# Gate weights before the inverse denominators, and their transposes and copy moved up, in phase two of a graph transformer layer

## Chip, core and metric

The kernel runs on one core of a Trainium2 chip. The metric is the device time of one launch in microseconds (us).

## What is computed

The reference is one layer over 12,500 nodes of 256 channels, with 12,500 of the edges used. Cut to what matters here:

```python
xn = layernorm(x)
x  = x + graph_attention(xn, edges) + linear_attention_mix(xn)      # elu+1 features, message, W1, relu, W2, layernorms
z  = layernorm(x)
gates = softmax(z @ gW + gb)                                         # 4 experts
topv, topi = top_k(gates, 2); topw = softmax(topv)                   # weights of the 2 kept experts
out = x + shared_mlp(z) + sum(topw * expert_mlp(z)[topi])
```

In the mix part each of 8 heads divides by a denominator, the dot product of its query features with the sum of its key features.

## The kernel before

Rows are handled in 25 groups of 500 nodes (`NG`, `GR`; 125 partitions by `T` = 4). Phase one (until about 250 us) builds the key/value sums and a table of transformed rows in DRAM. Phase two goes over the groups in a software pipeline, written out by hand for each engine as `phase2(i, par, a, b, c)`. In step i, part `a` is the attention part of group i, part `b` is W1 and W2 of the mix for group i-1, and part `c` is the feed-forward part (shared network, four experts, gates) of group i-2. All three run in steps 2 to 24; step 25 has b and c, step 26 has c alone. Steps 3 to 24 are mostly a hardware loop of two steps a turn. Each engine runs its own instructions in order, and only semaphores tie the engines together. Matrix products are split into three fp32r matmuls (L222 to L224), a high by high, a high by low and a low by high one; the "low" tiles (`h_lo`, `e_lo`, `s_lo`, `z_lo`) are subtractions, most of them on GpSimd (POOL) through the helper `low` (L1349).

The names that matter:

- **VectorE (DVE)**, part a and c of a step in this order: `p2_feature` (L1007, L1009), the softmax inputs (`soft_chain_in`), `compare` (ranks the four gate logits, L1092 to L1099), `soft_chain_out` (L1079 to L1083, signals `gates`), `one_over_den` (L1126 to L1132: add epsilon, reciprocal, split in two, signals `den_rows`), `top_weights` (L1108 to L1120: mask the exponentials, sum, reciprocal, multiply, split, write to `scale_rows`, signals `gate_rows`), row statistics `bn_y` (L902), the product of the query features with the inverse denominators (L1203, signals `q_den`), their low part `z_lo` (L1207), and later the product of the expert outputs with the expanded gates (L1217).
- **ScalarE (ACT)**: relu passes (L789, L790) of the four experts, then the exponential `top_exp` of the gates (L859), the high part `z_hi` of the scaled query features (L863, waits for `q_den`), the relu passes of `s2` (L789, L790; signals `s2_relu`), and for the two halves of the experts' second layer a relu (L873); `copy_scales` (L795, PSUM to `scaleT`) stands between these two.
- **TensorE (PE)**: `p2_den` (L492, denominators), W2 in two pairs of tiles (`w2_pair`), the expansion of the inverse denominators (L638, waits for `den_rows`), sW2, the first half of eW2, the four transposes of `scale_rows` (`transpose_scales`, L564, waits for `gate_rows`), the second half of eW2, the expansion of the gates (L662, waits for `scaleT` and `s2_relu`), the message matmuls (wait for `qz`, that is for `z_lo`), half of W1 for the next step, and the output matmuls.
- **POOL**: gathers of table rows (L1343, L1345), `h_lo`, `s_lo`, a sum into `base`, more gathers, `e_lo` for two pairs of experts, `s_lo` for s2, and small statistics.

The order on VectorE before:

```python
soft_chain_out(i, a, c)
if a: one_over_den(i)
if c: top_weights(i)
```

Of the kernel before, what the change touches and what calls it, by code (L numbers as in the profile page):

```python
# [53 lines left out]
def gps_layer(nc, A):  # L54

    ctx = ExitStack()
    with ctx:
# [353 lines left out]
        def _(pe):  # L411
# [144 lines left out]
            def phase2(i, par, a=True, b=True, c=True, started=False):  # L556
# [3 lines left out]
                def transpose_scales():  # L560
                    if due(i - 1):
                        pe.wait_ge(S["gate_rows"], i - 1)
                    for j in range(T):
                        last = pe.transpose(psum[:, 5, j * R:(j + 1) * R], scale_rows[:, j, :], ident[0:R, 0:R])  # L564
                    last.then_inc(S["scale_t"], 1)
# [65 lines left out]
                if b:  # L631
                    for pair in range(2) if c else (1,):
                        w2_pair(i, pair, c)
                if a:
                    pe.wait_ge(S["den_rows"], i + 1)
                    for q in range(CK):
                        for j in range(T):
                            last = pe.matmul(psum[:, 6 + q, j * P:j * P + R + 1], den_sel[:, q, j, :], rdenT[:],  # L638
                                             start=True, stop=True)
                        last.then_inc(S["dx"], 1)  # L640
                if c:
                    if due(i - 1):
                        pe.wait_ge(S["s1_lo"], i - 1)
                    if due(4 * (i - 1)):
                        pe.wait_ge(S["e1_relu"], 4 * (i - 1))
                    hidden("sW2", 0, 0, 4, (s1_hi, s1_lo)).then_inc(S["s2_mm"], 1)
                    for q in range(2):
                        if due(2 * (i - 2) + q + 1):
                            pe.wait_ge(S["e1_lo"], 2 * (i - 2) + q + 1)
                        for m in range(2):  # L650
                            e = 2 * q + m
                            last = split_mm(pe, colT(2 + q), (wslice(w_hi, "eW2", e), wslice(w_lo, "eW2", e)),
                                            (e1_hi[:, e, :], e1_lo[:, e, :]), m == 0, m == 1)
                        last.then_inc(S["e2_mm"], 1)
                        if q == 0:
                            transpose_scales()
                    if due(i - 1):
                        pe.wait_ge(S["scaleT"], i - 1)
                    if due(i - 1):
                        pe.wait_ge(S["s2_relu"], i - 1)  # L660
                    for q in range(2):
                        last = pe.matmul(colT(4 + q), gate_sel[:, q, :], scaleT[:], start=True, stop=True)  # L662
                    last.then_inc(S["gb"], 1)
# [46 lines left out]
        def _(act):  # L710
# [91 lines left out]
            def phase2(i, par, a=True, b=True, c=True, started=False):  # L802
                if b:
                    if due(i):
                        act.wait_ge(S["mt"], i)
                    act.activation(mT_hi[:], colT(0, 2), ACT.Copy).then_inc(S["mT_hi"], 1)
                if c:
                    if due(i - 1):
                        act.wait_ge(S["rs_z"], i - 1)
                    if due(i - 2):  # L810
                        act.wait_ge(S["zt"], i - 2)
                    normalize(row_z, lambda j: xmid[par][:, j, :], LZ, "z_norm")
                if b:
                    if due(i - 2):
                        act.wait_ge(S["e2_lo"], i - 2)
                for o in range(2):
                    if b:
                        relu_split(relu[0][:, o, :], h_hi[:, o, :], 4 + o, h_bias[:, o:o + 1],
                                   4 * (i - 1) + o + 1, "h_mm", "h_relu")
                    if c and o == 0:  # L820
                        if due(i - 1):
                            act.wait_ge(S["zt"], i - 1)
                        act.activation(z_hi[:], colT(0, 2), ACT.Copy).then_inc(S["z_hi"], 1)
                if b:
                    if due(2 * (i - 2)):
                        act.wait_ge(S["e1_lo"], 2 * (i - 2))
                    for o in range(2, 4):
                        relu_split(relu[1][:, o - 2, :], h_hi[:, o, :], 4 + o, h_bias[:, o:o + 1],
                                   4 * (i - 1) + o + 1, "h_mm", "h_relu")
                if c:  # L830
                    if due(i - 2):
                        act.wait_ge(S["s2_lo"], i - 2)
                    for o in range(2):
                        relu_split(relu[2][:, o, :], s1_hi[:, o, :], 5 if o == 0 else 0, s1_bias[:, o:o + 1],
                                   2 * (i - 2) + o + 1, "s1_mm", "s1_relu")
                        if o == 0:
                            act.wait_ge(S["lg_mm"], i - 1)
                            act.activation(logitsT[:], colT(1), ACT.Copy).then_inc(S["lg"], 1)
                if a and not started:
                    p2_exp(i)  # L840
                if c:
                    for e in range(EXPERTS):
                        if e == 0:
                            if b:
                                act.wait_ge(S["h_lo"], 2 * (i - 1) + 1)
                            else:
                                act.wait_ge(S["e2_lo"], i - 2)
                        if e == 2:
                            if b:
                                act.wait_ge(S["h_lo"], 2 * (i - 1) + 2)  # L850
                            else:
                                act.wait_ge(S["e1_lo"], 2 * (i - 2))
                        relu_split(relu[e // 2][:, e % 2, :], e1_hi[:, e, :], 1 + e, e1_bias[:, e:e + 1],
                                   4 * (i - 2) + e + 1, "e1_mm", "e1_relu")
                        if e == 2:
                            soft_exp(i, a, c)
                    if due(i - 1):
                        act.wait_ge(S["gates"], i - 1)
                    act.activation(top_e[:], soft_e[:, 0, :, :], ACT.Exp).then_inc(S["top_exp"], 1)  # L859
                if a:  # L860
                    for q in range(CK):
                        act.wait_ge(S["q_den"], 2 * i + q + 1)
                        act.activation(z_hi[:, q, :], qf[:, q, :], ACT.Copy).then_inc(S["qz_hi"], 1)  # L863
                if c:
                    if due(i - 1):
                        act.wait_ge(S["s1_lo"], i - 1)
                    relu_split(relu[2][:, 0, :], s2_hi[:], 4, s2_bias[:, 0:1], i - 1, "s2_mm", "s2_relu")
                    if due(2 * (i - 2) + 1):
                        act.wait_ge(S["e1_lo"], 2 * (i - 2) + 1)
                    for q in range(2):  # L870
                        if due(2 * (i - 2) + q + 1):
                            act.wait_ge(S["e2_mm"], 2 * (i - 2) + q + 1)
                        act.activation(relu[0][:, q, :], colT(2 + q), ACT.Relu,  # L873
                                       bias=e2_bias[:, q:q + 1]).then_inc(S["e2_relu"], 1)
                        if q == 0:
                            copy_scales(i)
                    for q in range(2):
                        if due(2 * (i - 2) + q + 1):
                            act.wait_ge(S["e2g"], 2 * (i - 2) + q + 1)
                        act.activation(h_hi[:, q, :], relu[0][:, q, :], ACT.Copy).then_inc(S["e2_hi"], 1)  # L880
                if a:
                    act.wait_ge(S["rs_m"], i + 1)
                    normalize(row_n, lambda j: rowt(6, j), LM, "m_norm")
                if a and not c:
                    soft_exp(i, a, c)
# [11 lines left out]
        def _(dve):  # L897
# [269 lines left out]
            def phase2(i, par, a=True, b=True, c=True, more=True, started=False):  # L1167
# [14 lines left out]
                if c:  # L1182
                    soft_chain_in(i, par, a, c)
                    dve.drain()
                    compare(i)
                    soft_chain_out(i, a, c)
                if a:
                    one_over_den(i)
                if c:
                    top_weights(i)  # L1190
                if b:
                    if due(2 * i - 1):
                        dve.wait_ge(S["w2"], 2 * i - 1)
# [240 lines left out]
```

## Time and profile before

| | |
|---|---|
| median of 3 runs | 1503.72 us (1503.57 to 1506.25) |
| profiled execution, own time | 1505.46 us |
| its span, first to last instruction | 1503.7 us |
| TensorE clock granted, mean | 0.986 |
| busy: PE / DVE / ACT / POOL | 1414.6 / 1151.3 / 759.2 / 953.5 us |
| DMA, mean over the span | 81 GB/s |

Read the rows this way: in a timeline row the numbers in front are the start and the time of the group in us from the span's start; "x2" is how many instructions the row merges; the brackets give how long the engine had been idle before and which instruction released it. TensorE matmuls overlap, so a row's duration is longer than the distance to the next one, and the distances are what counts.

### The profile page before, as it was taken

The page shows a single profiled execution, that of the slowest core. Times are in us where ns is not written, and L with a number is a line of the kernel's source. Part 1 is how long each engine was busy: PE and PEld are TensorE (multiplying, and loading weights), DVE is VectorE, ACT ScalarE, POOL GpSimd, SP SyncE. Part 2 cuts the span into 40 slices and gives each one's busy share as a digit, 9 for nine tenths or more (in the row PEclk, how much of TensorE's full clock was granted, in tenths as well). Part 3 has the DMA queues.
Part 4 walks back from the last instruction along what each step waited for, and adds up shares of the span by engine and source line. Part 5 has one row for each costly group of instructions (what it writes and reads, how often), then busy time and mean ns, then how long its engine had stood idle before and what let it go on. Part 6 is the DMA issues. An engine that isn't in the chain of part 4 may idle for free.

```text
span 1503.7 us, 26952 instructions
## 1 busy us (share of the span) xinstructions
PE 1414.6 (94%) x9032; PEld 1279.9 (85%) x9032; DVE 1151.3 (77%) x2565; ACT 759.2 (50%) x1339; POOL 953.5 (63%) x873
## 2 busy tenths in 40 slices
PE   5999999679999999999999999999999999999986
PEld 5999999568888888888888888888888888888875
DVE  6777778558878878787788877788777887878873
ACT  4555555235554445644556445554455445554453
POOL 5777775566775666656676567755677556675452
PEclk9999999899999999999999999999999999999998
DMA  5787765121220212202122112211122111220000
GB/s 175 254 266 230 226 217 194 53 60 49 70 70 23 64 52 69 65 24 62 56 69 62 28 48 69 69 41 48 48 69 69 31 55 52 69 67 24 14 14 14
DMA packets 71630, 121.81 MB, mean 81 GB/s; under 512 B 38053, under 2 KB 42786, under 8 KB 71598
## 3 DMA queue, kind: packets, MB, share of 16 engines
q1 hardware_dynamic: 55598, 108.00, 22.7%
q0 software_dynamic: 16000, 13.43, 4.1%
q8 instruction: 14, 0.23, 0.1%
q14 instruction: 18, 0.15, 0.0%
HBM read 69.47 MB, written 51.70 MB: 81 GB/s over the span
## 4 chain that ended last, share of the span: by engine, by line
PE 62%; DVE 21%; ACT 6%; issue 5%; DVEq 4%; POOL 1%; POOLq 1%; DMA 0%; SPq 0%; ACTq 0%
PE psum L222 18%; PE psum L224 18%; PE psum L223 18%; DVE top_e L1108 6%; PE psum L419 4%; DVE qf L1007 2%; DVE qf L1203 2%; ACT qf L775 2%; DVEq L1056 2%; DVE psum L1128 1%; PE psum L662 1%; ACT relu L789 1%; ACT relu L873 1%; ACT s_hi L790 1%; DVE bn_y L902 1%
## 5 line engine op out<-in xcount | busy, mean ns | idle before, releaser
L1349 POOL TENSOR_TENSOR s_lo<-relu,s_hi 128x1000 fp32r<-128x1000 f32 (+1 forms) x50 | 89.9, 1797 | 150.5 <-ACT s_hi L790 150.5
L222 PE MATMUL psum<-w_hi,h_hi 128*125 128x256 f32 x600 | 172.5, 287 | 5.1 <-DVE h_lo L1229 3.7
L224 PE MATMUL psum<-w_hi,h_lo 128*125 128x256 f32 x600 | 170.1, 283 | 0.0
L223 PE MATMUL psum<-w_lo,h_hi 128*125 128x256 f32 x600 | 169.6, 283 | 0.0
L1343 POOL DMA_INDIRECT xg<-table_xt,idx x100 | 124.7, 1247 | 55.1 <-issue 55.1
L863 ACT ACTIVATE z_hi<-qf 128x500 fp32r<-128x500 f32 x50 | 30.2, 622 | 232.2 <-DVE qf L1203 224.3
L1349 POOL TENSOR_TENSOR h_lo<-relu,h_hi 128x1000 fp32r<-128x1000 f32 x50 | 127.4, 2567 | 29.8 <-ACT h_hi L790 29.8
L1146 DVE SCALAR_TENSOR_TENSOR base<-xb,rn,b_bc 125x256 f32<-125x256 f32 x100 | 144.6, 1486 | 0.3
L1345 POOL DMA_INDIRECT ag<-table_al,idx x100 | 121.3, 1213 | 30.5 <-issue 30.5
L222 PE MATMUL psum<-z_hi,w_hi 128*128 128x500 f32 x300 | 119.8, 399 | 2.3 <-DVE z_lo L1177 2.3
L222 PE MATMUL psum<-xT_hi,w_hi 128*128 128x500 f32 x300 | 120.5, 402 | 1.3 <-ACT h_hi L790 1.3
L1349 POOL TENSOR_TENSOR e_lo<-relu,e_hi 128x1000 fp32r<-128x1000 f32 x50 | 116.1, 2348 | 3.3 <-ACT e_hi L790 2.7
L223 PE MATMUL psum<-xT_lo,w_hi 128*128 128x500 f32 x300 | 117.8, 393 | 0.0
L224 PE MATMUL psum<-xT_hi,w_lo 128*128 128x500 f32 x300 | 117.5, 392 | 0.0
L223 PE MATMUL psum<-z_lo,w_hi 128*128 128x500 f32 x300 | 117.4, 391 | 0.0
L222 PEld LDWEIGHTS psum<-w_hi,h_hi 128*125 128x125 f32 x600 | 112.2, 187 | 6.0 <-DVE h_lo L1229 4.1
L224 PE MATMUL psum<-z_hi,w_lo 128*128 128x500 f32 x300 | 116.9, 390 | 0.0
L714 ACT ACTIVATE row_n<-psum,nm_m,rs_m 125x256 f32<-125x256 f32 x100 | 48.4, 565 | 131.4 <-POOL nm_m L1286 131.4
L224 PEld LDWEIGHTS psum<-w_hi,h_lo 128*125 128x125 f32 x600 | 112.9, 188 | 0.0
L223 PEld LDWEIGHTS psum<-w_lo,h_hi 128*125 128x125 f32 x600 | 112.9, 188 | 0.0
L1108 DVE SCALAR_TENSOR_TENSOR top_e<-rank,top_e 125x16 f32<-125x16 f32 x25 | 91.3, 3650 | 4.4 <-issue 3.8
L1319 POOL TENSOR_TENSOR k_lo<-kf,k_hi 125x1024 fp32r<-125x1024 f32 x25 | 63.0, 2521 | 40.7 <-DVE k_hi L956 40.7
(231 smaller groups left out, 4754.1 us busy)
## 6 DMA issues: line engine op xcount, KB each, us to landing
xb<-in_x SPq DMA_DIRECT2D x50, 448.0 KB
xT_hi_table<-x1T_hi SPq DMA_DIRECT2D x25, 500.0 KB
xT_lo_table<-x1T_lo SPq DMA_DIRECT2D x25, 500.0 KB
xT_hi<-xT_hi_table SPq DMA_DIRECT2D x25, 500.0 KB
xT_lo<-xT_lo_table SPq DMA_DIRECT2D x25, 500.0 KB
table_xt<-xts SPq DMA_DIRECT2D x25, 455.0 KB
out<-xmid SPq DMA_DIRECT2D x25, 448.0 KB
xb<-in_x SPq DMA_DIRECT2D x50, 52.0 KB
```

The lines of the kernel that those rows point to most:

```text
L222: pe.matmul(out, wh, xh, start=first, stop=False)
L223: pe.matmul(out, wh, xl, start=False, stop=False)
L224: return pe.matmul(out, wl, xh, start=False, stop=last)
L419: last = pe.transpose(psum[:, b + c, j * R:(j + 1) * R], src[:, j, c * P:(c + 1) * P], ident[0:R, 0:R])
L714: act.activation(out[:, j, :], src(j), ACT.Identity, bias=nm[which][:, j:j + 1], scale=rs[which][:, j:j + 1]).then_inc(S[done], 1)
L863: act.activation(z_hi[:, q, :], qf[:, q, :], ACT.Copy).then_inc(S["qz_hi"], 1)
L1108: stt(top_e[:], rank[:], float(TOPK), top_e[:], ALU.is_lt, ALU.mult)
L1146: last = stt(base[:, j, :], xb[par][:, j, :], rn2[par][:, 0, j:j + 1], b2_bc[:], ALU.mult, ALU.add)
L1319: ptt(k_lo[par][:], kf[par][:], k_hi[par][:], ALU.subtract).then_inc(S["k_split"], 1)
L1343: pool.indirect_dma_start(xg[par][:, j, :], None, table_xt.ap(), bass.IndirectOffsetOnAxis(idx[par][:, 1, j:j + 1], 0)).then_inc(S[f"gath{ ...
L1345: pool.indirect_dma_start(ag[par][:, j, :], None, table_al.ap(), bass.IndirectOffsetOnAxis(idx[par][:, 0, j:j + 1], 0)).then_inc(S[f"gath{ ...
L1349: ptt(out, src, hi, ALU.subtract).then_inc(S[done], 1)
```

## The change

Three things move in phase two, and nothing is added or taken away. On VectorE `top_weights` comes right behind `soft_chain_out` and ahead of `one_over_den`. On TensorE the four transposes of the gate rows move from between the two halves of eW2 to right behind W2, ahead of the wait for `den_rows`. On ScalarE the copy of the transposed rows moves from between the two relus of the experts' second layer to right behind the exponential of the gates, ahead of `z_hi`.

```diff
@@ TensorE, phase2
                     for pair in range(2) if c else (1,):
                         w2_pair(i, pair, c)
+                if c:
+                    transpose_scales()
                 if a:
                     pe.wait_ge(S["den_rows"], i + 1)
@@
                         last.then_inc(S["e2_mm"], 1)
-                        if q == 0:
-                            transpose_scales()
@@ ScalarE, phase2
                     act.activation(top_e[:], soft_e[:, 0, :, :], ACT.Exp).then_inc(S["top_exp"], 1)
+                if c:
+                    copy_scales(i)
                 if a:
                     for q in range(CK):
                         act.wait_ge(S["q_den"], 2 * i + q + 1)
@@
                                        bias=e2_bias[:, q:q + 1]).then_inc(S["e2_relu"], 1)
-                        if q == 0:
-                            copy_scales(i)
@@ VectorE, phase2
                     soft_chain_out(i, a, c)
+                    top_weights(i)
                 if a:
                     one_over_den(i)
-                if c:
-                    top_weights(i)
```

## Rows read from the trace of the kernel before

**Rows 1.** Page, part 4: the chain that ended last, shares by engine and line.

```profile
PE 62%; DVE 21%; ACT 6%; issue 5%; DVEq 4%; POOL 1%; POOLq 1%; DMA 0%; SPq 0%; ACTq 0%
```

**Rows 2.** Waits of PE from 240 us to the end: total us, times, longest.

```profile
PE psum L662 <- ACT scaleT L795: 34.3, 23, 1.5
```

**Rows 3.** Timeline of PE in one step, from the end of W2.

```profile
977.17 1.01 PE L638 MATMUL psum<-rdenT,den_sel 128*128 128x126 f32 x8
978.01 0.44 PE L222 MATMUL psum<-s_hi,w_hi 128*128 128x500 f32 x1
...
980.77 0.59 PE L564 MATMUL psum<-ident,scale_rows 125*128 125x125 f32 x4
...
982.33 0.39 PE L224 MATMUL psum<-e_hi,w_lo 128*128 128x500 f32 x1
984.26 0.72 PE L662 MATMUL psum<-scaleT,gate_sel 128*128 128x500 f32 x2 [1.54 <-ACT scaleT L795]
984.83 0.28 PE L222 MATMUL psum<-g_hi,z_hi 128*125 128x256 f32 x1
```

**Rows 4.** Timeline of DVE in the same step.

```profile
970.49 0.19 DVE L1083 TENSOR_TENSOR soft_e<-soft_e,soft_s 125x32 f32<-125x32 f32 x1
971.67 0.30 DVE L1126 TENSOR_SCALAR psum<-psum 128x125 f32<-128x125 f32 x1 [0.99 <-issue]
...
973.43 0.29 DVE L1132 TENSOR_TENSOR rdenT<-psum,rdenT 64x125 fp32r<-64x125 f32 x1
973.91 4.12 DVE L1108 SCALAR_TENSOR_TENSOR top_e<-rank,top_e 125x16 f32<-125x16 f32 x1 [0.18 <-issue]
...
979.26 0.17 DVE L1120 TENSOR_TENSOR scale_rows<-top_e,top_hi 125x16 f32<-125x16 f32 x1
...
980.13 1.24 DVE L1203 TENSOR_TENSOR qf<-qf,psum 128x500 f32<-128x500 f32 x2
```

**Rows 5.** Timeline of ACT in the same step.

```profile
971.02 0.21 ACT L859 ACTIVATE top_e<-soft_e 125x16 f32<-125x16 f32 x1
980.83 1.21 ACT L863 ACTIVATE z_hi<-qf 128x500 fp32r<-128x500 f32 x2 [9.59 <-DVE qf L1203]
981.94 0.67 ACT L789 ACTIVATE relu<-psum,s_bias 128x500 f32<-128x500 f32 x1
...
983.62 0.59 ACT L795 ACTIVATE scaleT<-psum 128x500 fp32r<-128x500 f32 x1
```

**Rows 6.** Timeline of POOL in the same step.

```profile
973.33 4.66 POOL L1349 TENSOR_TENSOR e_lo<-relu,e_hi 128x1000 fp32r<-128x1000 f32 x2
983.24 1.24 POOL L1349 TENSOR_TENSOR s_lo<-relu,s_hi 128x500 fp32r<-128x500 f32 x1 [5.26 <-ACT s_hi L790]
```

**Rows 7.** Line L1108 over the whole kernel: duration in ns, min/median/max.

```profile
L1108 DVE SCALAR_TENSOR_TENSOR top_e<-rank,top_e x25: 174/4117/4218, 356.1 to 1483.3; 125x16 f32<-125x16 f32 x25
```

**Rows 8.** Timeline of POOL and DVE beside a gather in the next step.

```profile
997.75 1.33 POOL L1343 DMA_INDIRECT xg<-table_xt,idx  x1 [0.60 <-issue]
...
998.56 1.05 DVE L1160 TENSOR_SCALAR gnn<-xg,soft_e,rn 125x64 f32<-125x64 f32 x4
```

**Rows 9.** Timeline of DVE and PE in steps 24, 25 and 26.

```profile
1402.24 0.19 DVE L1083 TENSOR_TENSOR soft_e<-soft_e,soft_s 125x32 f32<-125x32 f32 x1
...
1404.91 1.01 PE L638 MATMUL psum<-rdenT,den_sel 128*128 128x126 f32 x8
...
1447.17 0.39 PE L222 MATMUL psum<-s_hi,w_hi 128*128 128x500 f32 x1
...
1449.46 0.17 DVE L1120 TENSOR_TENSOR scale_rows<-top_e,top_hi 125x16 f32<-125x16 f32 x1
...
1485.92 0.96 PE L564 MATMUL psum<-ident,scale_rows 125*128 125x125 f32 x4 [2.29 <-DVE scale_rows L1120]
...
1489.19 0.76 PE L662 MATMUL psum<-scaleT,gate_sel 128*128 128x500 f32 x2
```

**Rows 10.** Busy times in a window: PE, PEld, DVE, ACT, POOL, granted clock, DMA.

```profile
1486.50:1489.20 2.70, 2.70 (x9) 2.19 (x8) 0.00 (x0) 0.59 (x1) 0.00 (x0) 0.50 0.00 0
```

## The prediction

> **What bounds the kernel now.** I read the page's chain first: TensorE holds 62% of it and VectorE 21% [rows 1]. So the end is set by TensorE for most of each step and by a chain on VectorE for the rest. I then asked the waits of PE alone, over the whole of phase two. One wait stands out: L662, the expansion of the gates, waits for `scaleT`, 23 times, 34.3 us in all [rows 2]. Last came one step on every engine. From the first L1108 at 356.1 to the one shown at 973.91 there are 13 steps, 47.5 us each [rows 4, 7], and they repeat within hundredths of a microsecond, so one step stands for 22 of them (2 to 23).
>
> On PE the step runs without a gap until the last eW2 matmul at 982.33; L662 comes at 984.26 and the message matmuls at 984.83 [rows 3]. Twelve matmuls of the same size take 980.77 - 978.01 = 2.76, or 0.23 each. Without a wait the message would begin at 982.33 + 3 x 0.23 = 983.02. The wait thus costs 984.83 - 983.02 = 1.8 us a step, a little more than the 1.54 in brackets, which counts from the modelled end of the last matmul.
>
> What is late is a chain on VectorE. L1108 works on 16 elements and takes 4.12 us [rows 4]; its median over 25 is 4117 ns and its minimum 174 [rows 7]. The engine does not need that time. It begins at 973.91, inside the two `e_lo` subtractions of POOL, which run from 973.33 to 977.99, and ends at 978.03 [rows 4, 6]. So an instruction of VectorE with two SBUF operands stands still while POOL subtracts. L1132, which has one operand in PSUM, starts at 973.43, inside the same subtraction, and takes 0.29 [rows 4]: it is not held. Behind L1108 come the rest of `top_weights` (until 979.26 + 0.17 = 979.43), `bn_y` and L1203 at 980.13 [rows 4]. ACT waits 9.59 us for L1203, then does `z_hi`, the relus of s2, a relu of e2 and last the copy of the scales from 983.62 to 984.21 [rows 5]. That releases L662.
>
> **The VectorE order.** L859 ends at 971.23 [rows 5]. `top_weights` can start 0.03 later, at 971.26. L1108 unblocked takes 0.17 [rows 7], and from its end to the end of L1120 it is 979.43 - 978.03 = 1.40 [rows 4]. That gives 972.83, which is 0.50 before `e_lo` starts at 973.33 [rows 6]. Both sides keep this distance: POOL and VectorE are both set off by TensorE's work earlier in the step, of which nothing changes. So the 4.1 us stall goes. `one_over_den` then runs from 972.85 and needs 973.72 - 971.67 = 2.05: `den_rows` comes at 974.9 instead of 973.7. It now lies beside `e_lo`, but none of its four instructions reads two SBUF operands, and L1132 shows such a one unheld. TensorE asks for it after W2 and the moved transposes, at 977.57, so 2.7 us of slack cover it. If the cover were gone, each microsecond of lateness would cost one.
>
> Row and rule: the stall row above fits what the Trainium skill says (page "SBUF — State Buffer", section "Who interferes with whom"): VectorE instructions with two SBUF inputs contend with a GpSimd instruction that reads SBUF, and the one that started first goes through. The same section also speaks against the change: casts and copies in SBUF in a two-port mode take the pair as well and can collide with GpSimd's writing of DMA descriptors, and the moved L1116 and L1119 are such. The page gives no price for a 16-element copy.
>
> From rows: `top_weights` will now run beside the gathers that end just before `e_lo`. No row has a copy beside a gather; the nearest is L1160, SBUF to SBUF, four in 1.05 us beside a gather of 1.33 [rows 8], so about 0.26 each. The bound from below is nothing, and from above one gather of 1.33 for the copies. I take nothing; the upper bound is the rival below.
>
> **The moved transposes and copy.** They wait for `gate_rows` (972.83), long past when PE reaches them at 977.17. Between 980.77 and the last eW2 matmul at 982.33 lie the transposes and five spacings, so they take 1.56 - 5 x 0.23 = 0.4 of PE's time, wherever they stand [rows 3]. The expansion of the denominators moves from 977.17 to 977.57. L1203 can start when half of it is through and has landed: 977.57 + 0.42 (half of the 0.84 to sW2) + about 0.3 = 978.3 instead of 980.13. The copy on ACT (0.59) fits at 977.8 to 978.4 in a 9.59 us idle stretch [rows 5]; behind its wait stands only `z_hi`, which needs L1203 anyway. `z_hi` follows L1203 by 0.70 as now: 979.0. The relus of s2 follow that by 1.11 and take 2 x 0.67 at most: `s2_relu` at 981.4 [rows 4, 5]. PE asks for it at 982.56, 1.1 us later. `z_lo` goes behind `z_hi` (until 980.2) half by half and ends about 980.9; PE wants it at 983.0. `s_lo` on POOL, which waits for `s2_relu` [rows 6], would start near 981.4, after `z_lo`, so these two don't meet. So L662 follows the last eW2 matmul directly. The later part of the step hangs on PE and shifts as a whole. No DMA issue is moved, and SP's and POOL's queues are passed by nothing. Gathers and loads have a step of slack.
>
> Sum for steps 2 to 23: 22 x -1.8 = -40 us. With only the bracketed 1.54 won it is -34.
>
> **The last three steps pay.** Step 24: POOL has no gathers there, `e_lo` runs early and delays the softmax instead, L1083 ends at 1402.43 [rows 9]. `gate_rows` comes at 1402.43 + 0.3 + 1.6 = 1404.3 and `den_rows` 2.05 later, at 1406.3, while PE is ready at 1404.91 + 0.4. It waits 1.0 there and loses its old wait at L662, the twenty-third of them (34.3 - 22 x 1.53 = 0.6, and 0.3 more as above): +0.1. Step 25: PE reaches sW2 at 1447.17, but the transposes now stand in front and `gate_rows` comes at 1449.63 [rows 9]: PE waits 2.5 us, +2.5, as the rest of the tail hangs on eW2. Step 26: the transposes wait until 1485.92 already, but with 12 matmuls done before. Now these come behind. From the transposes to L662 there were 3.27 us for 4 transposes and 6 matmuls at a clock of 0.50, its lower level of 1.2 GHz [rows 9, 10]. At the upper level the same takes 0.4 + 6 x 0.23 = 1.8. With 18 matmuls it is 4.5 at the upper level and 4.5 x 3.27 / 1.8 = 8.2 at the lower. So L662 moves by +1.2 to +4.9; the output matmuls behind it may give back up to 1.5 where the clock has risen by then. I take +2.5, nearer to the row with the low clock. Together +5, from +1.5 to +8; should the clock fall in step 25 too, 18 matmuls there at twice the spacing add 4.
>
> **Sum.** -40 + 5 = -35 us. Against the profiled execution's own 1505.46 that gives 1470.5. That execution lay 1.7 above the median of the runs, so I put the median at **1469 us**, -2.3%.
>
> **Rivals.**
>
> *POOL gets the port first (slower).* If one of L1108 to L1120 is still to start when `e_lo` does at 973.33, it stands until 977.99. The margin is 0.67 for the start of L1120 (972.66). The copies held by a gather, up to 1.33, would use it up. Then `gate_rows` comes at 978.2, the transposes end at 978.6, `den_rows` comes at 980.25, the expansion starts at 980.3 and sW2 at 981.15. Eighteen matmuls bring PE to L662 at 985.3 and two more spacings to the message at 985.75, against 984.83: +0.9 a step, x 22 = +20, +5 for the tail: 1529. For it: the margin is thin, and no row has copies beside gathers. Against it: L1160 beside one, and steps that repeat so closely. Chance 0.08.
>
> *A second wait takes over.* L662 or the message could find `s2_relu` or `z_lo` late, if L1203 is held or starts later than I put it. From 1.1 us of lateness it costs; with 2 us a step it takes 0.8 of the 1.8 and leaves -22 + 5: 1487. Against it: the brackets of ACT show idleness before `z_hi` [rows 5]. Chance 0.08.
>
> *It doesn't do what it says.* If the 4 us belong to the first instruction that waits for `top_exp`, and not to POOL, the stall moves with it: L1108 would end at 975.4, `den_rows` comes at 975.4 + 1.4 + 2.05 = 978.85, and PE waits 1.3 there in place of 1.8 at L662: 22 x -0.5 + 5 = -6, 1498. The minimum of 174 ns [rows 7] speaks against it. Chance 0.04.
>
> **Numbers.** A change under 0.2% (3 us) can't be told from none here. My forecast has 0.80, its own range 1465 to 1482: -34 + 12 above, -40 + 1.5 below. To hold 8 in 10 I reach towards the second-wait case: 1461 to 1487. Faster 0.88, same 0.03, slower 0.09.
>
> **What would show it.** Right: L1108 at 0.17 us in steps 2 to 23, L662 without idle time before it, steps 45.7 us apart, L638 0.4 later relative to W2, a new PE wait at L564 near 2.5 us in step 25 and one at L638 in step 24. Wrong: a DVE line of 4 us elsewhere in `top_weights`, PE idle before L564 or L638 in every step, or a low clock through more of the tail.

## The result: slower by 2.6%, and what the profile after shows

| | before | changed |
|---|---|---|
| median | 1503.67 us (4 runs, 1503.57 to 1506.25) | 1543.58 us (4 runs, 1541.8 to 1545.52) |
| ratio, 95% interval | | 1.0261 [1.0244, 1.0279] |
| span of the profiled execution | 1503.7 us | 1541.5 us |
| mean granted TensorE clock | 0.986 | 0.977 |

The chain of the page, which answers [rows 1], has moved towards TensorE; its line of lines now has "DVE scale_rows L1119 8%"; before, L1108 had 6%.

```profile
PE 67%; DVE 18%; ACT 8%; issue 4%; POOL 2%; DVEq 1%; POOLq 0%; DMA 0%; SPq 0%; ACTq 0%
```

The waits of PE over phase two answer [rows 2] (total us, times, longest):

```profile
PE psum L640 <- DVE rdenT L1132: 31.9, 24, 2.2
PE psum L564 <- DVE scale_rows L1120: 27.4, 24, 5.9
```

The wait at L662 is gone, as forecast. Two others have come: for the gate rows at the transposes, and for the inverse denominators right behind them. Together they are 59 us. The wait at L662 was 34.3; the two new lines had one wait each before too, 4.5 together.

VectorE in one step (start, duration), to be read against [rows 4], and POOL in the same step against [rows 6]:

```profile
990.96 0.18 DVE L1108 SCALAR_TENSOR_TENSOR top_e<-rank,top_e 125x16 f32<-125x16 f32 x1 [0.69 <-ACT top_e L859]
...
991.96 0.18 DVE L1116 CAST top_hi<-top_e 125x16 fp32r<-125x16 f32 x1
992.21 5.37 DVE L1119 COPY scale_rows<-top_hi 125x16 f32<-125x16 f32 x1
...
997.66 0.28 DVE L1126 TENSOR_SCALAR psum<-psum 128x125 f32<-128x125 f32 x1
...
999.40 0.29 DVE L1132 TENSOR_TENSOR rdenT<-psum,rdenT 64x125 fp32r<-64x125 f32 x1
```

```profile
990.16 1.21 POOL L1342 DMA_INDIRECT xg<-table_xt,idx  x1 [0.30 <-issue]
991.68 1.21 POOL L1344 DMA_INDIRECT ag<-table_al,idx  x1 [0.30 <-issue]
992.91 4.62 POOL L1348 TENSOR_TENSOR e_lo<-relu,e_hi 128x1000 fp32r<-128x1000 f32 x2
```

L1108 takes 0.18, so that stall did go. But the first copy L1119 now takes 5.37 us for 16 elements. It starts 0.70 before `e_lo` by the records and ends with it (997.58 against 997.53). `one_over_den` follows only then, so `den_rows` comes at 999.7 (the end of L1132), and PE stands still twice, 0.86 and 1.31 us (idle time in brackets):

```profile
997.79 0.65 PE L564 MATMUL psum<-ident,scale_rows 125*128 125x125 f32 x4 [0.86 <-DVE scale_rows L1120]
999.75 1.11 PE L640 MATMUL psum<-rdenT,den_sel 128*128 128x126 f32 x8 [1.31 <-DVE rdenT L1132]
```

The steps are not alike any more. Two of three take 48.4 us, 0.87 more than the 47.5 before; every third takes 50.0. In the longer ones TensorE's granted clock goes to 0.50, its lower level of 1.2 GHz, right behind the two pauses. The windows of such a step (columns as in [rows 10]):

```profile
650.00:656.00 6.00, 4.02 (x33) 3.58 (x31) 5.78 (x7) 0.59 (x1) 4.01 (x2) 1.00 0.02 1
656.00:658.00 2.00, 1.78 (x10) 1.68 (x11) 1.96 (x5) 0.31 (x1) 0.00 (x0) 0.80 0.00 0
658.00:660.00 2.00, 2.00 (x6) 1.59 (x5) 1.90 (x5) 0.89 (x2) 0.00 (x0) 0.50 0.00 0
660.00:662.00 2.00, 2.00 (x9) 1.58 (x9) 0.66 (x5) 1.47 (x3) 0.65 (x1) 0.85 0.00 0
662.00:664.00 2.00, 2.00 (x13) 1.76 (x12) 0.21 (x1) 1.13 (x2) 1.19 (x4) 1.00 0.00 0
```

Added up between the starts of L1007 in steps 2 and 24, the 22 steps take 1077.3 us against 1045.5. Of the 31.8, 22 x 0.87 = 19 are the waits and 8 x 1.6 = 13 the clock in eight steps. What follows step 24's L1007 is 117.6 against 112.0, +5.6. With 0.3 in front this is the 37.8 by which the span grew.

### The profile page after: what moved, and what is told of

Same layout as the page of the kernel before. It is cut to its first block, busy times and chain, and to the rows that moved or that the text cites. A ratio compares the mean times of both kernels' runs of the same rounds, so it can differ in the third digit from the quotient of the medians.

```text
span 1541.5 us, 26952 instructions
## 1 busy us (share of the span) xinstructions
PE 1432.3 (93%) x9032; PEld 1293.6 (84%) x9032; DVE 1178.1 (76%) x2565; ACT 768.1 (50%) x1339; POOL 953.1 (62%) x873
## 4 chain that ended last, share of the span: by engine, by line
PE 67%; DVE 18%; ACT 8%; issue 4%; POOL 2%; DVEq 1%; POOLq 0%; DMA 0%; SPq 0%; ACTq 0%
PE psum L222 19%; PE psum L223 19%; PE psum L224 19%; DVE scale_rows L1119 8%; PE psum L419 4%; ACT e_hi L790 3%; ACT relu L789 3%; DVE qf L1007 2%; PE psum L640 2%; DVE psum L1128 1%; PE psum L571 1%; PE psum L570 1%; PE psum L688 1%; PE psum L662 1%; POOL ag L1344 1%
## 5 line engine op out<-in xcount | busy, mean ns | idle before, releaser
L1119 DVE COPY scale_rows<-top_hi 125x16 f32<-125x16 f32 x50 | 122.1, 2483 | 2.1 <-issue 0.2
L795 ACT ACTIVATE scaleT<-psum 128x500 fp32r<-128x500 f32 x25 | 14.7, 587 | 176.7 <-PE psum L564 176.7
```

The source lines that it names most:

```text
L1119: dve.tensor_copy(scale_rows[:, :, at:at + EXPERTS], top_hi[:])
```

## The experiments

Two questions stand: what holds the copy, and whether the moves are worth anything once it isn't held. "The port" stands below for whatever POOL and VectorE share here: in [rows 4, 6] an instruction of VectorE with two SBUF operands stood still while POOL subtracted. Theory G is the trigger that the prediction's first rival named: a copy from SBUF to SBUF is held by the gather beside it, and `e_lo` takes over when the gather ends. Theory P: `e_lo` itself, ready behind the gather, has the port some time before its recorded start.

**The VectorE move alone.** Transposes and scale copy stay at their old places.

```diff
                     soft_chain_out(i, a, c)
+                    top_weights(i)
                 if a:
                     one_over_den(i)
-                if c:
-                    top_weights(i)
```

> Only the VectorE move is made; transposes and scale copy stay where they were before. In the changed kernel the first copy L1119 of the gate rows took 5.37 us of its step and both gate_rows and den_rows came late. Theory G (a copy from SBUF to SBUF is held by the gather beside it until the gather ends, and then by the e_lo subtractions that start at once): nothing on VectorE changes, so L1119 stays at 5.4 us, den_rows is as late as in the changed kernel, and PE waits once, at the expansion of the denominators, about 2.8 us, in place of 0.9 + 1.3. The transposes are then no longer hidden in a wait (+0.4 a step), the tail is free of its new waits (about -5 us): 1540 to 1552. If the moved transposes were what costs, and not the VectorE order, this one would be near 1504 or below.

1564.0 us, ratio 1.0399 [1.0381, 1.0418]. L1119 is held as in the changed kernel, and PE waits once a step, at the denominators:

```profile
864.12 1.11 PE L638 MATMUL psum<-rdenT,den_sel 128*128 128x126 f32 x8 [2.85 <-DVE rdenT L1132]
```

So the VectorE order alone is enough for a loss. It is 12 us above the expected range: steps take 48.8, 50.4 or 51.7 us, and over 52 us that hold one of 51.7 the granted clock is 0.93, over one of 48.8 it is 1.00. Of the steps 2 to 23, 15 are longer than 48.8; in the changed kernel the clock fell in 8.

**The transposes and the scale copy alone.** VectorE keeps the old order; PE and ACT have the new one.

Against the changed kernel:

```diff
-                    top_weights(i)
                 if a:
                     one_over_den(i)
+                if c:
+                    top_weights(i)
```

> Only the moves on PE and ACT are made; VectorE keeps the old order, so L1108 stalls behind e_lo as before (4.1 us). gate_rows comes 2.3 us after PE reaches the transposes, so PE waits 2.2 us there and not 1.5 at L662. Both theories: +0.5 us a step and about +5 in the tail, 1517 to 1525; if the longer wait also brings the TensorE clock to its lower level in some steps, as in the changed kernel, up to 1535.

1590.04 us, ratio 1.0564 [1.0546, 1.0581]: the wait is as expected, the time is not. PE waits 2.13 us for the gate rows, and in each of the steps 2 to 23 the clock falls right behind it:

```profile
770.90 1.10 PE L564 MATMUL psum<-ident,scale_rows 125*128 125x125 f32 x4 [2.13 <-DVE scale_rows L1120]
```

The window behind it:

```profile
770.80:779.00 8.20, 8.10 (x28) 7.06 (x29) 4.48 (x13) 3.69 (x6) 1.37 (x2) 0.58 0.00 0
```

The transposes take 1.10 there in place of 0.59 [rows 3], the window behind them runs at 0.58, and steps come at 51.2 us, 3.7 more than before, of which the longer wait explains 0.6 (2.13 for 1.54) and the clock the rest. By itself this part is worse than the whole change.

**The copies with two operands.** The changed kernel; the same values are written by an operation that reads two SBUF operands.

```diff
                 for at in (0, 64):
-                    dve.tensor_copy(scale_rows[:, :, at:at + EXPERTS], top_hi[:])
+                    tt(scale_rows[:, :, at:at + EXPERTS], top_hi[:].bitcast(F32), top_hi[:].bitcast(F32), ALU.max)
```

> The changed kernel, but the two copies of the gate rows are written as a maximum of the tile with itself (two SBUF operands, same values), because L1108 and L1114, which have two SBUF operands, took 0.18 beside the gather. Theory G: the two take about 0.17 each or less, L1120 ends about 0.15 us before e_lo starts in half the steps and 0.4 in the others, PE has no wait at L564, L640 or L662, steps come at 45.7 us in place of 49.0: 22 x 3.3 = 72 less than 1543.6, 1472. Rival P (POOL claims the operands before its recorded start, so any VectorE instruction that starts in the last 0.8 us before e_lo is held, whatever its form): the first of the two is held 5.4 us and the time is 1540 to 1548.

1543.27 us, ratio 1.0258 [1.0241, 1.0275], the same as the change. The first of the two starts 0.70 before `e_lo` and is held just as the copy was:

```profile
991.98 1.21 POOL L1344 DMA_INDIRECT ag<-table_al,idx  x1 [0.30 <-issue]
993.22 4.65 POOL L1348 TENSOR_TENSOR e_lo<-relu,e_hi 128x1000 fp32r<-128x1000 f32 x2
```

The two operations in that step, min/median/max in ns:

```profile
L1119 DVE TENSOR_TENSOR scale_rows<-top_hi x2: 162/2776/5391, 992.5 to 997.8; 125x16 f32<-125x16 f32 x2
```

L1114, which reads two operands too and starts with this last gather, took 0.2. L1108, also with two operands, starts about 0.8 us into the gather before it, behind which stands another gather and not `e_lo`, and took 0.17; in the changed kernel it is the same (0.18 at 990.96, beside the gather of 990.16). So a gather by itself does not hold an instruction with two operands, and one that starts 0.53 into the gather ahead of `e_lo` is held. Theory G falls for this form; for copies the next run decides.

**`e_lo` waits for the gate rows.** The changed kernel with one wait more.

```diff
                 if c:
+                    if due(i - 1):
+                        pool.wait_ge(S["gate_rows"], i - 1)
                     for n in range(2):        # e_lo
```

> The changed kernel, but POOL waits for gate_rows before e_lo, so the subtractions can't start before the copies are through. Theory G: the first copy is still held, but only to the end of the gather, 0.7 us instead of 5.4; e_lo starts about 0.3 us later than before, which PE does not notice; PE waits vanish and the time is 1472. Rival P: nothing claims the operands here, the first copy takes 0.17 at once; the time is the same 1472. The length of L1119 tells them apart: 0.7 or 0.17.

1463.87 us, ratio 0.9729 [0.9713, 0.9745]. Every step takes 45.7 us, and PE has no wait at L564, L640 or L662 in steps 2 to 23. POOL in one step, with a gather from 995.49 to 996.70:

```profile
995.49 1.21 POOL L1344 DMA_INDIRECT ag<-table_al,idx  x1 [0.30 <-issue]
996.72 4.65 POOL L1348 TENSOR_TENSOR e_lo<-relu,e_hi 128x1000 fp32r<-128x1000 f32 x2
```

The two copies of that step:

```profile
L1119 DVE COPY scale_rows<-top_hi x2: 170/174/177, 995.9 to 996.0; 125x16 f32<-125x16 f32 x2
```

The first starts 0.41 behind the start of the gather and takes 0.17. In the changed kernel one that started 0.53 behind it (992.21) took 5.37, and in the steps between one that started 0.41 behind took 5.50. In every second step of this run the first copy starts 0.54 behind the gather's start and takes 0.175. So the gather is not what holds it, and neither is the distance to `e_lo`, which starts right behind the gather here too. What differs is that `e_lo` had to wait: standing ready behind the gather, it has the port before its recorded start, and when it waits on a semaphore, it has not.

The gather does hold a copy that starts later in it. In every second step of this run the second copy starts 0.62 in, takes up to 0.577 and ends with the gather (493.00 is both copies, the second from 493.08 to 493.65):

```profile
492.45 1.21 POOL L1344 DMA_INDIRECT ag<-table_al,idx  x1 [0.30 <-issue]
493.00 0.65 DVE L1119 COPY scale_rows<-top_hi 125x16 f32<-125x16 f32 x2
```

Both theories put the time at 1472; it is 8 us less, nearly all of it in the tail: what follows step 24's L1007 takes 110.55 us against 117.6 in the changed kernel.

**A drain before `e_lo`.** The changed kernel; no wait for VectorE, but POOL drains first.

```diff
                 if c:
+                    pool.drain()
                     for n in range(2):        # e_lo
```

> The changed kernel with a drain on POOL between the last gather and e_lo, and no wait for VectorE. Theory P (as the run with two-operand copies left it: e_lo, when nothing keeps it back, claims the second SBUF port about 0.7 us before its recorded start, during the gather ahead of it): after a drain it can't be sent ahead, the first copy L1119 takes 0.17 to 0.6 us, gate_rows comes before e_lo, PE loses all waits in steps 2 to 23 and the time is 1464 to 1468. Rival: the claim is not made ahead by e_lo but the gather itself holds the copy to its end and e_lo follows at once; then the copy takes 0.7, and is through only if the drain leaves a gap after the gather. If the drain changes nothing (5.4 us copies, 1543), e_lo claims the port though it is behind a drain, or the drain ends with the gather.

1471.46 us, ratio 0.9772 [0.9757, 0.9787]. The copies take 0.17 and at most 0.58, steps 45.7 us. The drain leaves POOL idle for 2 us:

```profile
949.64 1.21 POOL L1344 DMA_INDIRECT ag<-table_al,idx  x1 [0.30 <-issue]
952.87 4.63 POOL L1348 TENSOR_TENSOR e_lo<-relu,e_hi 128x1000 fp32r<-128x1000 f32 x2 [2.02 <-issue]
```

So it moves `e_lo` 2.0 us away from the gather, and can't tell an early claim from mere distance. Most of the 7.6 us above the run with the wait lie in the tail, where PE waits 5.9 us at L564 in step 26 as in the changed kernel.

**Shorter by two instructions.** The changed kernel without sum and reciprocal of the gate weights (L1110, L1112), so the weights are not normalised (`top_s` is set to one ahead of phase two); POOL is untouched.

> The changed kernel without the sum and the reciprocal of the gate weights (L1110, L1112; the weights are not normalised, so the output differs), each followed by a drain: the copies start 0.5 us earlier, 1.2 before e_lo, and L1120 1.04 before it. Nothing is changed on POOL. Theory P: only what starts within about 0.75 of e_lo is held, so nothing is held and the time is 1464. Rival (a copy beside a gather is held whatever its distance to e_lo): 1543.

1469.36 us, ratio 0.9764 [0.9749, 0.9779], steps of 45.7. All 50 copies:

```profile
L1115 DVE COPY scale_rows<-top_hi x50: 160/176/216, 355.3 to 1446.2; 125x16 f32<-125x16 f32 x50
```

Half a microsecond earlier is enough for steps 2 to 23. Most of the 5 us above the expected 1464 lie in the tail with its waits of 1.8 and 5.1 at the transposes.

**Shorter by one instruction.** Only the reciprocal (L1112) is left out.

> The changed kernel without the reciprocal of the gate weights (L1112 and its drain; the output differs): the first copy starts 0.95 us (in every second step 1.08) before e_lo, L1120 0.79 (0.92) before. In the changed kernel a copy 0.70 and 0.83 before it was held, with two instructions less nothing 1.0 and more before it was. Theory P with a claim about 0.8 before the recorded start: L1120 is held in every second step or its whole chain just gets through; the time is 1464 to 1470 if it gets through, about 1505 if it is held in every second step. It places the edge of the claim.

1516.75 us, ratio 1.0083 [1.0067, 1.0098]. 14 waits at L564 are left of 24, 12 of them in steps 2 to 23. The time is above the expected 1505: in 9 of these 12 steps the granted clock falls as well, for 1.6 or 3.1 us each. Two steps side by side, the first held, the second not:

```profile
881.73 5.55 DVE L1117 COPY scale_rows<-top_hi 125x16 f32<-125x16 f32 x1
...
882.61 2.35 POOL L1346 TENSOR_TENSOR e_lo<-relu,e_hi 128x1000 fp32r<-128x1000 f32 x1
...
931.61 0.17 DVE L1118 TENSOR_TENSOR scale_rows<-top_e,top_hi 125x16 f32<-125x16 f32 x1
...
932.52 2.37 POOL L1346 TENSOR_TENSOR e_lo<-relu,e_hi 128x1000 fp32r<-128x1000 f32 x1
```

The instruction that starts 0.88 before `e_lo` is held, the one that starts 0.91 before is not. Over steps 2 to 23 of the changed kernel, of the VectorE move alone, of the two-operand copies and of the two shortened kernels, the held ones start 0.68 to 0.90 ahead and the passing ones 0.91 or more. This is the edge: the port is gone about 0.9 us ahead of the recorded start, a third of a microsecond into the gather. It is further ahead than the 0.8 that I had expected.

**The old order with the wait.** The kernel before, none of the three moves, and the wait of `e_lo` for `gate_rows`.

> The kernel before, all three orders as they were, with one line more: POOL waits for gate_rows before e_lo. L1108 then meets no subtraction and takes 0.17; gate_rows comes at +1.6 behind den_rows, and e_lo starts 2.7 us later than before and ends 2.6 us later, which still is ahead of the second half of eW2 by 0.5. L1203 comes 2 us earlier, the scale copy no longer waits behind z_hi, and the wait at L662 is gone. Theory (the port, not the order of the moved parts, is what costs): 45.7 us a step, 1462 to 1466 in all. Rival (the moves are needed for the gain): PE still waits at L662, or for e_lo before the second half of eW2: 1475 to 1500.

1463.98 us, ratio 0.9725 [0.9711, 0.9738].

```profile
951.23 0.29 DVE L1132 TENSOR_TENSOR rdenT<-psum,rdenT 64x125 fp32r<-64x125 f32 x1
951.70 0.17 DVE L1108 SCALAR_TENSOR_TENSOR top_e<-rank,top_e 125x16 f32<-125x16 f32 x1 [0.18 <-issue]
...
953.11 0.17 DVE L1120 TENSOR_TENSOR scale_rows<-top_e,top_hi 125x16 f32<-125x16 f32 x1
...
953.46 4.63 POOL L1349 TENSOR_TENSOR e_lo<-relu,e_hi 128x1000 fp32r<-128x1000 f32 x2 [2.38 <-DVE scale_rows L1120]
...
960.35 0.61 PE L662 MATMUL psum<-scaleT,gate_sel 128*128 128x500 f32 x2
```

L1108 is at 0.17, POOL gives up 2.38 us of a stretch in which it was idle 5.26 later anyway [rows 6], and L662 has no bracket. The whole gain that the change was forecast to bring comes without it.

**The VectorE move with the wait**, transposes and scale copy at their old places.

> The VectorE move and the wait of e_lo for gate_rows, with the transposes and the scale copy at their old places. Theory (only the port matters): L1119 at 0.25 for both, no wait at L662, 45.7 us a step, 1462 to 1466, the same as with the moves and the same as the old order with the wait. If the moves of transposes and copy matter once the port is free: PE waits at L662 again, 1475 or more.

1464.74 us, ratio 0.9741 [0.9726, 0.9755], steps of 45.7, no wait at L662. With the port free, each of the three placings gives the same step.

**The tail, two trials.** First the changed kernel with the wait, and in the steps without part a the transposes and the scale copy back at their old places (one of the places, cut):

```diff
-                if c:
+                if a and c:
                     transpose_scales()        # and copy_scales; without a: at the old place
```

> The changed kernel with POOL waiting for gate_rows before e_lo, and in the last two steps (no part a) the transposes and the scale copy at their old places. Steps 2 to 23 as in the run with the wait alone (45.7 us). There PE waited 3.4 us at the transposes of step 26 after a pause; at the old place 12 matmuls come first. Theory: 2 to 4 us less than 1463.9, about 1461. If the tail is bound by the chain to gate_rows either way, within 1 us of 1463.9.

1464.33 us, ratio 0.9732 [0.9719, 0.9746]: nothing is gained. PE waits 2.71 us for `e_lo` in step 26 where it had waited 3.37 for the gate rows. Then the old order with the wait only where part a runs:

> The old order with the wait of e_lo for gate_rows only in steps that have part a (2 to 24), so that in steps 25 and 26, where PE waited 2.7 us for e_lo, the subtractions go as early as before. Theory: steps at 45.7 us, and the tail is the one of the kernel before with its wait for gate_rows of 2.3 in step 26: within 2 us of 1464, since what e_lo gains VectorE loses.

1463.65 us, ratio 0.9737 [0.9724, 0.9751], the same again. In the steps without part a one wait of PE is traded for another of much the same length; why they come out even was not followed further.

## Why the prediction was wrong

**What failed is one step, in "The VectorE order":** `top_weights` ends at 972.83, "which is 0.50 before `e_lo` starts", "so the 4.1 us stall goes". The distance was measured to the recorded start of `e_lo`. The runs with one and with two instructions less place the port's loss 0.9 us ahead of that start. By the forecast's own times L1120 would start 0.67 ahead, the second copy 0.76 and the first 0.84, so three instructions lay inside these 0.9 us all along. The first copy was the one held: it starts 0.83 ahead, in every second step 0.70, and takes 5.4 to 5.5 us in place of the 4.1 saved. The forecast's own signs of being wrong came: a VectorE line of over 4 us elsewhere in `top_weights`, PE idle at L564 and L640 in steps 2 to 23, and a low clock in eight of them.

**A row misread on the way.** "I take nothing" for copies beside a gather rested on L1160, "four in 1.05", "so about 0.26 each" [rows 8]. The four overlap, so the group's time divided by four is not the time of one. The first of them starts 0.81 into the gather, takes 0.51 and ends with the gather:

```profile
L1160 DVE TENSOR_SCALAR gnn<-xg,soft_e,rn x1: 508/508/508, 998.6 to 998.6; 125x64 f32<-125x64 f32 x1
```

So the trace before did show an SBUF-to-SBUF instruction held by a gather. This is not what cost the time, since the held copies start earlier in the gather than that, but it spoke for the rival that was given 0.08.

**The slower rival was right in its place and in its size, and wrong in its trigger.** It put PE's loss at 0.9 a step; two of three steps show 0.87. It wanted a copy delayed by a gather to use the margin up. No such delay was needed, and the run with two-operand copies shows that the form does not matter for what `e_lo` holds. Its total of 1529 missed the clock: 13 of the 14.6 us between it and 1543.6. The chance of 0.08 was far too small for a margin of half a microsecond between two engines where no row showed an instruction close ahead of `e_lo`.

**The waits after the stall.** Right: with the port free, `den_rows` is covered, none of the instructions of `one_over_den` is held beside `e_lo`, L662 follows without a gap, and steps are 45.7 us apart, as the five runs with the wait, the one with the drain and the one shortened by two instructions have it. The 1.8 us for the wait at L662 is right: 47.5 - 45.7. The second rival, `s2_relu` or `z_lo` late, shows in none of them.

**The transposes and the copy.** Costed at 0.4 wherever they stand, with 4.3 us to spare. That held only while `gate_rows` was early. Once it is late, the transposes in front turn its lateness into a pause of PE ahead of work that was ready: alone they cost 86 us, of which, by the steps, 0.6 us a step is the longer wait and 3.1 the clock.

**The tail.** +5 was forecast, 5.6 measured in the changed kernel, though in other parts: PE waits 0.81 at the denominators in step 24 and 2.31 at the transposes in step 25, close to the 1.0 and 2.5 forecast, and 5.9 in step 26.

**The third rival**, that the stall belongs to the first instruction that waits for `top_exp`, is refuted by L1108 at 0.18.

The Trainium skill (page "SBUF — State Buffer", section "Who interferes with whom") says that whichever of the two engines issues first gets the shared pair for its whole instruction, and the other is blocked. The runs agree that the loser waits to the end: the held copy ends at 997.58, `e_lo` at 997.53. The prediction wrote "started first", and that can't be read off the recorded starts: here VectorE instructions whose recorded start was 0.68 to 0.90 us earlier lost. The same section's rule that copies collide with descriptor writing fits the copies and L1160 that a gather held to its end, but it did not decide the time: up to 0.54 us into a gather a copy took 0.17.

## What to carry to other kernels

When a small VectorE instruction takes microseconds, look at what POOL runs, and order the two by a semaphore instead of by timing: here one wait on POOL, in a stretch where it had 5 us to spare, brought 2.7%, and moving the VectorE work to where it seemed to fit cost 4.0% alone and 2.6% with the two other moves. A margin between two engines that share a port counts only if it is larger than the uncertainty of the recorded starts, 0.9 us here behind a gather. And before work is put in front of a wait on TensorE, ask what stands behind it if the awaited data is late, since the pause may cost the clock as well. Last, the time of a merged group of overlapping instructions says nothing on the single one; ask for the longest of them.

## What the runs showed of the hardware that was not expected

- POOL's subtraction, when it is ready behind a gather of 1.21 us, keeps VectorE instructions with two SBUF operands, and copies, from finishing before it ends if they start in the last 0.9 us before its recorded start; those that start earlier pass. Behind a semaphore wait it does not. That the claim is made while the gather still runs is the reading that fits all of these; what happens inside POOL was not seen.
- A gather by itself holds copies and the one-operand L1160, if they start late in it, until it ends. In the run where `e_lo` waits, in every second step the second copy starts 0.62 behind the gather's start and ends 1.18 behind it (maximum 577 ns); copies that start up to 0.54 behind pass. It does not hold instructions with two SBUF operands: L1108 starts 0.8 into a gather in the changed kernel and takes 0.18.
- A drain on POOL behind a gather took 2.0 us.
- TensorE's clock was seen to fall behind pauses of this size. With one of 1.5 us a step the granted clock stayed at 1.00. With 0.86 and 1.31 close together it fell to the lower level in 8 of 22 steps, with 2.85 in 15, and with 2.13 in all 22, where the step of 51.2 us is 3.1 longer than its wait explains. So the length of a pause alone does not tell in how many steps it falls.
